# The set-up of a transformer-block kernel in another order: modulation and first rows first, the second attention's weights after the first keys

## The reference

```python
def adaln(x, t, w, b):
    scale, shift = split(t @ w + b, 2)
    return layernorm(x) * (1.0 + scale) + shift
h1 = adaln(x, t, norm1_w, norm1_b)
x = mha(h1, h1, attn1_wq, attn1_wk, attn1_wv, attn1_wo, attn1_bo) + x
h2 = adaln(x, t, norm2_w, norm2_b)
x = mha(h2, context, attn2_...) + x              # 16 heads of 64
h3 = adaln(x, t, norm3_w, norm3_b)
x = glu_ff(h3, ff_w1, ff_b1, ff_w2, ff_b2) + x
# around it: x + block(layernorm(x)), then x + experts(layernorm(x)), top 2 of 8
```

## Time and profile before

| | us |
|---|---|
| median of 3 runs | 2274.69 |
| the profiled execution's own time | 2251.97 |
| its span, first to last instruction | 2250.1 |
| set-up: first PE instruction of it to last DVE split | 9.02 to 38.38 |
| first keys on PE start | 55.03 |
| first `peak` on DVE starts | 64.43 |

### The profile page before, as it was taken

The page is one execution under the profiler, slowest core; times in us unless marked ns, Lnnn a source line. Parts: engine busy times, 40 slices in busy tenths (PEclk is TensorE's granted clock), DMA queues, the critical chain, the costliest instruction groups (busy, mean ns, idle before and its releaser), DMA issues. The chain is left out here.

```text
span 2250.1 us, 36649 instructions
## 1 busy us (share of the span) xinstructions
PE 2105.5 (94%) x10284; PEld 1280.5 (57%) x10285; DVE 1263.8 (56%) x3230; ACT 1289.2 (57%) x2456; POOL 822.7 (37%) x1022
## 2 busy tenths in 40 slices
PE   4899999999999999999999999999999788799996
PEld 3455555555555555555555555555555456577775
DVE  3454556575656565656565666656644734445454
ACT  3565666666656666656666666666655534444432
POOL 1122223333333334242433342424232434546654
PEclk8999999999999999999999999999999999999998
DMA  4001111111111111111212111121113111112265
GB/s 139 24 24 48 47 33 48 43 48 43 47 47 47 43 47 43 47 52 41 58 33 56 43 47 52 38 52 38 47 47 106 36 55 47 51 47 66 63 206 171
DMA packets 134430, 127.73 MB, mean 57 GB/s; under 512 B 14649, under 2 KB 108377, under 8 KB 134298
## 3 DMA queue, kind: packets, MB, share of 16 engines
q1 hardware_dynamic: 125018, 108.03, 17.3%
q0 software_dynamic: 9280, 18.28, 2.4%
HBM read 86.63 MB, written 40.67 MB: 57 GB/s over the span
## 5 line engine op out<-in xcount | busy, mean ns | idle before, releaser
L1721 POOL TENSOR_TENSOR pr<-pr,sm 128x512 f32<-128x512 f32 x256 | 262.8, 1045 | 760.2 <-DVE sm L1310 760.2
L732 PE MATMUL ps<-tt,V 128*128 128x512 f32 x1024 | 501.7, 594 | 4.5 <-ACT tt L1035 4.5
L1035 ACT ACTIVATE kp<-ps 128x512 f32<-128x512 f32 x512 | 295.8, 600 | 198.6 <-PE ps L269 195.2
L1300 DVE TENSOR_REDUCE mx<-ps 128x8 f32<-128x512 f32 x256 | 176.9, 691 | 335.2 <-PE ps L689 332.0
L689 PE MATMUL ps<-kp,hf 128*64 128x256 f32 x2048 | 279.3, 395 | 11.7 <-DVE pr L1303 8.7
L269 PE MATMUL ps<-hk,M 128*128 128x512 f32 x768 | 250.5, 450 | 27.2 <-DVE pr L1303 25.1
L1035 ACT ACTIVATE tt<-ps 128x512 f32<-128x512 f32 x512 | 273.6, 588 | 2.2 <-PE ps L719 2.2
L269 PE MATMUL ps<-cT,M 128*128 128x512 f32 x768 | 268.5, 473 | 0.0
L689 PEld LDWEIGHTS ps<-kp,hf 128*64 128x64 f32 x2048 | 125.5, 137 | 202.5 <-DVE pr L1303 130.2
L1035 ACT ACTIVATE pt<-ps 128x512 f32<-128x512 f32 x256 | 153.5, 600 | 151.8 <-PE ps L701 151.8
L1063 ACT ACTIVATE pr<-pr 128x512 f32<-128x512 f32 x256 | 161.7, 631 | 136.4 <-DVE pr L1303 134.7
(11 more groups left out here) (221 smaller groups left out, 3047.9 us busy)
## 6 DMA issues: line engine op xcount, KB each, us to landing
mod<-emb_s SPq DMA_DIRECT2D x96, 256.0 KB, 4.2
xr<-rows_s SPq DMA_DIRECT2D x144, 66.0 KB
cb<-y_s SPq DMA_DIRECT2D x32, 256.0 KB, 4.0
x_in<-in_x_dram SPq DMA_DIRECT2D x16, 256.0 KB, 4.4
xn_s<-x_in SPq DMA_DIRECT2D x16, 256.0 KB, 2.0
res<-xn_s SPq DMA_DIRECT2D x16, 256.0 KB, 2.7
c_in<-in_ctx_dram SPq DMA_DIRECT2D x16, 256.0 KB, 4.8
y_s<-res SPq DMA_DIRECT2D x16, 256.0 KB, 2.0
```

The costliest lines, as they stand in the source:

```text
L732: mm = nc.tensor.matmul(psO[:], Vw[a][:, g * HG + head_at(h), :], tt[:, h, :], start=(g == 0 and h == 0), stop=(g == 1 and h == HG - 1))
L1035: return nc.scalar.activation(o, i, ACT.Copy)
L1300: nc.vector.tensor_reduce(mx[:, p % 2, :], heads(psS[p % 2][:]), AX_X, ALU.max).then_inc(max_done, 1)
L1721: tensor(v, v, sm[:, p, :].unsqueeze(2).broadcast_to([P, HG, 64]), ALU.mult).then_inc(prob_done, 1)
```

## The change

The list of tiles now begins with C and the three E tiles (NE = 4), then the fourteen tiles of attention 1 (up to N1 = 18), then the fourteen of attention 2 and R (NSU = 33). Each engine's loop over the list is cut into a function `setup(lo, hi)` that is called in pieces. SP loads `cond`, the norm weights and biases (under a new semaphore `ld_n`) and the first rows first, then the weights; it writes `emb_s` as soon as the E tiles are evicted, and waits for the end of the whole set-up just before the rounds. From tile N1 on the banks are 0, 1, 2, 4 in place of 0 to 3, since bank 3 belongs to the first keys. POOL no longer waits for `emb_s`. In the staging area `wT` is moved, and the raw weights of attention 1 are laid out first.

```diff
-        tiles += [("R",), ("C",), ("E", 0), ("E", 1), ("E", 2)]
+        tiles = [("C",), ("E", 0), ("E", 1), ("E", 2)]
+        NE = len(tiles)
+
+        def attention_tiles(a):
+            return ([("T", a, k, g) for k in range(3) for g in range(H // 8)]
+                    + [("M", a, g) for g in range(H // 4)] + [("V", a, g) for g in range(H // 4)])
+
+        tiles += attention_tiles(0)
+        N1 = len(tiles)
+        tiles += attention_tiles(1) + [("R",)]
         NSU = len(tiles)
+
+        def setup_bank(n):
+
+            return SR[n % 4] if n < N1 else [psum[i] for i in (0, 1, 2, 4)][(n - N1) % 4]
...
         @block.sync
         def _(sp):
+            sp.dma_start(rawc[:], cond_d).then_inc(ld_n, 16)
+            for n in range(3):
+                sp.dma_start(rawn[:, n, :], t_in[f"L0_xcond_norm{n + 1}_w"]).then_inc(ld_n, 16)
+                sp.dma_start(brow[:, n, :], t_in[f"L0_xcond_norm{n + 1}_b"].unsqueeze(0)).then_inc(ld_n, 16)
+            sp.dma_start(x_in[:], x_v[0]).then_inc(ld_x, 16)
             for a in range(2):
...
+            sp.dma_start(rawr[:], t_in["L0_ffn_wqkv"]).then_inc(ld_m, 16)
+            sp.wait_ge(su_act, NE)
+            sp.wait_ge(su_dve, NE)
+            sp.dma_start(emb_s, emb[:].rearrange("p n k -> p (n k)")).then_inc(emb_w, 16)
...
-            sp.wait_ge(su_act, NSU + 2)
-            sp.wait_ge(su_dve, NSU + 2)
-            sp.dma_start(emb_s, emb[:].rearrange("p n k -> p (n k)")).then_inc(emb_w, 16)
             sp.wait_ge(emb_w, 16)
...
-            new_x(0)
             load_mod(0, 0)
             ln_x(0)
+            sp.wait_ge(su_act, NSU + 2)
+            sp.wait_ge(su_dve, NSU + 2)
             rounds(sp, round_)
...
+            setup(0, N1)
+            pe.wait_ge(su_dve, N1)
             pe.wait_ge(mods[0], 2)
             turn4(psM, hx[0], lambda t: h1[:, t, :])
             for h in range(HG):
                 keys(0, 0, h)
+            setup(N1, NSU)
+            pe.wait_ge(su_dve, NSU)
             rounds(pe, lambda i: [slot(i, u) for u in range(4)])
...
+            setup(0, N1)
             ln_hi(0, 0)
             for h in range(HG):
                 keys_hi(0, 0, h)
+            setup(N1, NSU)
+            act.wait_ge(ld_m, 48)
+            copy(W1[:, 0, :], raw1[:]).then_inc(su_act, 1)
+            copy(W2[:, 0], raw2[:]).then_inc(su_act, 1)
+            act.wait_ge(ld_b, 64)
             rounds(act, lambda i: [slot(i, u) for u in range(4)])
...
+            setup(0, NE)
             ln1_stats(0)
+            setup(NE, N1 - H // 4)
             ln1(0)
+            setup(N1 - H // 4, N1)
             ln_lo(0, 0)
+            setup(N1, NSU)
+            dve.wait_ge(su_act, NSU + 1)
+            tensor(W1[:, 1, :], raw1[:], f32(W1[:, 0, :]), ALU.subtract).then_inc(su_dve, 1)
+            dve.wait_ge(su_act, NSU + 2)
+            tensor(W2[:, 1], raw2[:], f32(W2[:, 0]), ALU.subtract).then_inc(su_dve, 1)
             rounds(dve, lambda i: [slot(i, u) for u in range(4)])
...
             pool.wait_ge(consts, 3)
-            pool.wait_ge(emb_w, 16)
```

More of the change, by code:

```diff
@@ L168, in sg @@
                     return sb(name, shape, dt, staging)
-                raw = [[sg(f"raw{a}{k}", [P, INNER]) for k in range(3)] for a in range(2)]
-                rawo = [sg(f"rawo{a}", [P, H // 2, D]) for a in range(2)]
+                raw, rawo = [], []
+                for a in range(2):
+                    raw.append([sg(f"raw{a}{k}", [P, INNER]) for k in range(3)])
+                    rawo.append(sg(f"rawo{a}", [P, H // 2, D]))
                 raw1 = sg("raw1", [P, 2 * DFF])
@@ L173, in pixart_block_moe @@
                 rawr = sg("rawr", [3 * E, D])
+                wT = [[sg(f"wT{a}{k}", [P, H // 2, P]) for k in range(3)] for a in range(2)]
                 rawn = sg("rawn", [P, 3, 2 * D])
@@ L176, in pixart_block_moe @@
                 rawc = sg("rawc", [B, D])
-                wT = [[sg(f"wT{a}{k}", [P, H // 2, P]) for k in range(3)] for a in range(2)]
                 condT = sg("condT", [P, B])
@@ L212, in pixart_block_moe @@
         ld_w = [sem(f"ld_w{a}") for a in range(2)]
-        ld_m = sem("ld_m")
+        ld_m, ld_n = sem("ld_m"), sem("ld_n")
         ld_b = sem("ld_b")
@@ L629, in _, with setup, setup_tile @@
             pe.wait_ge(identity, 2)
-            for n, tile in enumerate(tiles):
-                ps = SR[n % 4]
+            def setup(lo, hi):
+                for n, tile in enumerate(tiles):
+                    if lo <= n < hi:
+                        setup_tile(n, tile)
+            def setup_tile(n, tile):
+                ps = setup_bank(n)
                 if n >= 4:
@@ L649, in _ @@
                 elif tile[0] == "R":
-                    pe.wait_ge(ld_m, 160)
+                    pe.wait_ge(ld_m, 48)
                     mm = nc.tensor.transpose(ps[:, 0:3 * E], rawr[:], ident[0:3 * E, 0:3 * E])
                 elif tile[0] == "C":
+                    pe.wait_ge(ld_n, 112)
                     mm = nc.tensor.transpose(ps[:, 0:B], rawc[:], ident[:])
@@ L1035, in copy, with setup, setup_copy @@
                 return nc.scalar.activation(o, i, ACT.Copy)
-            for n, tile in enumerate(tiles):
-                ps = SR[n % 4]
+            def setup(lo, hi):
+                for n, tile in enumerate(tiles):
+                    if lo <= n < hi:
+                        setup_copy(n, tile)
+            def setup_copy(n, tile):
+                ps = setup_bank(n)
                 act.wait_ge(su_pe, n + 1)
@@ L1055, in _ @@
                 op.then_inc(su_act, 1)
[L1056 to L1059, removed]
             def exp(i, u, p):
@@ L1267, in _, with setup, setup_rest @@
             nc.vector.memset(eps[:], EPS).then_inc(consts, 1)
-            for n, tile in enumerate(tiles):
-                ps = SR[n % 4]
+            def setup(lo, hi):
+                for n, tile in enumerate(tiles):
+                    if lo <= n < hi:
+                        setup_rest(n, tile)
+            def setup_rest(n, tile):
+                ps = setup_bank(n)
                 dve.wait_ge(su_act, n + 1)
@@ L1287, in _ @@
                 op.then_inc(su_dve, 1)
[L1288 to L1291, removed]
             def heads(ap):
```

## The result

The kernel after takes 2264.51 us, the median of 5 runs (2259.67 to 2266.39), against 2274.70 for the kernel before in the same series: 10.2 us less by the medians, ratio 0.9951 with a 95% interval of 0.9939 to 0.9963, which is 8.4 to 13.9 us. Forecast were 2262.2 us, 12.5 less.

A forecast was written before the change was run, and what follows sets the result against it. The prediction took the kernel as bound by PE's matmuls in the rounds, behind a set-up chain without overlap; eight steps moved the first maximum from 64.43 to about 51.9, so 2274.69 - 12.5 = 2262.2 us, range 2257.2 to 2267.7.

The forecast's parts named there:

- step 4: Modulation: `emb_s` write waits behind all weights until about 17.5 us; `mod` issued at 19.5, landed at 24.4.
- step 1: Start of SP's queue: eight small loads ahead cost 3.3 us, so the first attention's weights land at 12.3.
- Step 2: C and E tiles as PE's first work: C starts at 6.1, E block takes 8.2 us, `emb` ready at 14.3.
- step 3: First attention's T and M tiles: 8.2 us, T tiles at full pace, DVE done at 21.9.
- step 5: Norm and `h` on DVE, done at 26.4; V copies behind them add 1.7 us, until 28.1.
- Steps 6 to 8: Transposes from 28.1, keys from 31.2 for 7.55 us, R done at 48.4, weight split, first maximum at about 51.9.
- A: Rival: in the set-up everything overlaps, `mod` lands by 21.5, first maximum about 47.2; 2258.7 us, chance 0.20.
- B: Rival: full queue or small biases hold back the modulation's write, `mod` at 28 to 29; gain 8, 2266.7 us, chance 0.13.
- C: Rival: first rounds give the saving back, waiting for a load at a fixed time; gain about 0, 2274.7 us, chance 0.06.
- D: Rival: PE's clock stays at the lower level through the whole set-up; 11.6 us slower, 2286.3 us, chance 0.03.
- Its split of the gain into parts: Set-up: 12.9 us from hidden latencies and 5.6 from E, less 3.3 for later weights and about 2.7 for waiting and copies.
- its last sign: Whole prediction is wrong if the first maximum is 12 us earlier and the end of the span is not.

The follow-up runs named there:

- late_mod: Kernel after with C and E behind the first attention's tiles and the modulation late, first keys still between the two attentions' tiles; ratio to before 0.9988.
- emb_early: Kernel after with the write of `emb_s` and load of `mod` issued ahead of the second attention's weights; ratio to the kernel before 0.9949.
- v_first: Kernel after with DVE's V copies of the first attention ahead of the norm of the first rows; ratio to the kernel before 0.9950.
- a2_first: Kernel after with the second attention's tiles and R ahead of the first keys again, modulation still early; ratio to the kernel before 0.9938.
- after_again: The kernel after unchanged, run again in a later series; 2243.11 us, ratio to the kernel before 0.9955.
- best: Kernel after with second attention's tiles before the first keys, DVE's norm and `h` in gaps, `h` transposed between second M and V tiles; ratio to before 0.9906.
- bias_late: Kernel after with the four small bias loads issued behind `mod`; one run, no ratio given, `mod` issued at 22.29 us against 22.25.
- before_again: The kernel before unchanged, profiled again for its stages; first maximum at 64.4 us, profiled span 2248.8 us.

## Why the prediction was right, and by how much it was off

The direction, the place and the chain were right. The gain was 10.2 us by the medians (8.4 to 13.9 by the interval) in place of 12.5, and 10.9 at the first maximum. By the prediction's own steps:

| step | forecast | profile of after |
|---|---|---|
| 1 first weight issued | 4.1 | 3.97 |
| 1 weights landed | 12.3 | 13.58 |
| 2 C starts, `emb` ready | 6.1, 14.3 | 5.21, 13.83 |
| 3 M tiles done on DVE | 21.9 | 23.37 |
| 4 `mod` issued, first used | 19.5, 24.4 | 22.25, 27.47 |
| 5 transposes of `h` | 28.1 | 30.72 |
| 6 keys start, length on PE | 31.2, 7.55 | 33.73, 7.49 |
| 7 R done | 48.4 | 50.52 |
| 8 first maximum | 51.9 | 53.57 |

1. The term that was mis-sized is step 4, by 3.1 us at the first use of `mod`: 2.75 until its issue and 0.3 from there. I let the queue's loads end at 17.5. Added up over the windows of after, and less the 384 KB of the write, the same bytes are through at about 20.1. There are two errors in this, the sum and the order. The sum: before, the queue still moved 191 GB/s between 17 and 18, and the 256 KB of `x_in` come on top. late_mod shows what that makes. It has the same loads, with the small ones behind the attention weights, and its queue is empty at about 18.4:

```profile
18.00:19.00 1.00, 1.00 (x17) 1.00 (x16) 0.98 (x3) 0.69 (x2) 0.00 (x0) 1.00 0.46 121
19.00:20.00 1.00, 1.00 (x12) 0.80 (x8) 0.71 (x2) 0.58 (x3) 0.00 (x0) 1.00 0.00 0
```

In after the window from 19 to 20 still has this:

```profile
19.00:20.00 1.00, 0.90 (x11) 0.94 (x12) 0.00 (x0) 0.00 (x0) 0.00 (x0) 1.00 1.08 337
```

So about 0.9 us of the error is the sum, and about 1.7 the order: with the small loads in front the queue moves 163 GB/s where it moved 410, which I had not counted. The order shows in step 1 too, where the weights landed 1.3 us late. `rawr`'s 2.22 us was a full queue, as I read it: SP's long issue now is that of `ff_w1` (4.27 us), while `cond` at the front took 0.39. That the write waits behind the weights was right, and emb_early shows it: 2.34 us from its issue to that of `mod` without the second attention's weights in front, 7.33 with them.

2. Step 2 had the E block at 8.2 us and it took 8.6. For the T tiles (step 3) I had taken full pace after some 5.4 us of PE work. They took 4.49 us, not 2.84: the E tiles had not brought PE to full pace. This cost nothing in the sum, because `mod` was later still.

3. The V copies on the path (step 5, forecast 1.7) were there and took 1.41; v_first takes them off. Steps 6 to 8 came out within 0.5 us each. With the V copies they gave back 1.4 of the 3.1 us lost at `mod`, so 1.7 was missing at the first maximum.

4. The sum had PE wait for the modulation, but I did not ask what could stand in that hole. PE's 6.13 us lie there because the second attention's tiles, which need no modulation, were put behind the keys. a2_first shows that this half of the change costs beside an early modulation (5.2 us at the first maximum against after, 3.9 in time against after_again, with the two smaller differences named there). late_mod's 4.9 us at the first maximum don't speak for it, since the early first rows and the write that no longer waits for the split account for them.

5. Of the rivals, A did not come (the write did wait), though best reaches 43.8, further than A's 47.2, by another order. B named the right place: `mod` landed at about 27.4, between the forecast and B's 28 to 29. SP did stand on its long issue (4.27 us for `ff_w1`) and issued `emb_s` at 14.92, 1.1 us after `emb` was ready, but that cost nothing by itself, since the write then stood behind the weights' bytes; the small biases, B's other cause, are out by bias_late. C fell: over six timed kernels the time won follows the time won at the first maximum to 2.2 us (10.9 and 11.1; 9.0 and 10.1; 11.3 and 11.3; 13.2 and 11.5; 16.1 and 14.0; 4.9 and 2.7; 20.7 and 21.2, two of them being the kernel after). D fell: the M and V tiles ran at their old pace (2.79 and 2.95 us), and only the first T tiles (4.49 us, against 2.78 for those of the second attention) and part of the keys at the lower one: their granted clock was 0.50 from 33.73 to 37, 0.74 in 37 to 38 and 1.00 behind that, and they took 7.49 us against 5.74 for the second eight.

6. Two smaller things in the prediction's text. Its split of the gain into parts (12.9 and 5.6, less 3.3 and 2.7) does not follow from its rows: from 38.47 to 51.95 it is 13.5, and the eight steps carry the forecast, not that split. And its last sign, wrong as a whole if the first maximum is 12 us earlier and the end of the span is not, came true by the letter in the first pair of profiles: the first maximum is 10.9 us earlier and the span 14.5 longer. The timed runs and the second profile of after (span 2241.3 us, against 2250.1 and 2248.8 for before) say otherwise.

The spans of the two first profiles differ that way because of a late stage. From the first scatter to the last of the experts' results it is 389 us before and 409 after; in after_again 387, in before_again 387. First the window of after, then of after_again:

```profile
2000.00:2050.00 50.00, 43.55 (x243) 32.89 (x242) 22.54 (x68) 19.63 (x54) 28.26 (x45) 0.91 0.19 55
```

```profile
2000.00:2050.00 50.00, 48.94 (x297) 38.48 (x296) 26.54 (x81) 23.09 (x65) 31.24 (x51) 1.00 0.24 66
```

The granted clock dipped there in the profile of after alone (0.91 in this window and 0.93 to 0.95 in the 100 us behind it; 0.97 to 1.00 in the other nine profiles). The timed runs of that series were all slower, the unchanged kernel's too (2274.70 against 2253.51 and 2254.3 later), so the level doesn't come from the change; whether from the chip or something else is open. The ratio of after to before is the same at both levels.

## What to carry to other kernels

A small transfer whose result something waits for belongs in front of the bulk loads of its queue (from the issue of `emb_s` to that of `mod` it was 2.34 us in emb_early, and 7.33 behind the weights in after), or its consumer must be placed where it is late anyway. Small loads at the very front were not free here either: the queue moved 163 GB/s between 3 and 4 us in place of 410, and ended, by the estimate above, about 1.7 us later. Before work is interleaved, list what each engine could do while the late operand is under way, and put all of that ahead of the first instruction that waits for it: the same early modulation was worth 10.1 us with PE waiting for it (after_again) and 21.2 with PE working through (best). A small step of an engine can go into the gaps that it has in another stage, as DVE's norm did in best (1.11 us at 19.96).

## What was not expected of the hardware

The E tiles did not bring PE to full pace, 2.84 us for six T tiles. In the kernel after C and E were PE's first work, 7.4 us of it between 5.21 and 13.20, and the first T tiles behind them still took 4.49 us (4.18 to 5.36 in the other kernels that start the same way). Where the same T tiles are PE's very first work, with no E tiles ahead, they took 4.42 (late_mod) and 5.35 (before).

Nor did the E tiles keep it there. In late_mod the granted clock fell from 0.98 to 0.50 in the middle of them, at about 22.5 us, with PE busy in each of the windows shown, and E matmul pairs went from 0.69 to 1.22 us; in before it fell at the end of the same tiles (0.54 in the half us from 35.0). A pause of 0.89 us stands in front of these tiles in late_mod. A pause of 1.02 us in front of the M tiles left those at their full pace of 2.79 us, so the pause alone is not the likely cause, but no run separates the two.

The profile's granted clock reads 1.00 from the first instruction on in every kernel here, while the matmul pairs of 7.38 and 8.53 in after take 1.22 us, as long as those at 0.50 in late_mod (23.17 to 25.47) and not the 0.69 of those at 1.00 there (21.61). In the windows of after up to its E tiles the 1.00 so doesn't fit the durations, and I go by the durations.

In a2_first the clock fell at 39.1 us, behind pauses of 0.85 and 1.90 us with only four transposes between them, and the keys began at the lower level. In best PE had no such pause (4.00 of 4 us busy in 32 to 36) and the keys ran at 1.00, in 6.17 us against 7.24. This is one profile of each.
